# A two-layer graph network on one core: the transposes of h move from TensorE to VectorE and a DRAM table

## The reference

```python
h = jnp.maximum(_layernorm(x, axis=-1), 0.0)       # 50000 x 256
agg = jax.ops.segment_sum(h[src], dst, num_segments=50000)
h = agg + h
h1 = h @ W1 + b1                                    # 256 -> 1024
mean = jnp.mean(h1, axis=0)
var = jnp.mean(jnp.square(h1 - mean), axis=0)
h1 = relu((h1 - mean) * rsqrt(var + 1e-05) * gamma + beta)
out = x + relu(h1 @ W2 + b2)                        # 1024 -> 256
```

## Time and profile before

| what | value |
|---|---|
| median of 3 runs | 3976.13 us (3973.02 to 3977.18) |
| the profiled execution, its own time | 3966.72 us |
| its span, first to last instruction | 3965.0 us |
| PE busy | 3512.4 us, 89% |
| DVE busy | 2160.1 us, 54% |
| ACT busy | 2164.0 us, 55% |
| POOL busy | 1039.5 us, 26% |
| mean granted clock of TensorE | 0.950 |

### The profile page before, as it was taken

How to read it: one execution, slowest core, us unless ns; L and a number is a source line. 1 busy time by engine, 2 the same in 40 slices (tenths; PEclk the granted TensorE clock), 3 DMA queues, 4 the chain that set the end, 5 groups by cost and what they waited for, 6 DMA issues and landing times.

```text
span 3965.0 us, 58120 instructions
## 1 busy us (share of the span) xinstructions
PE 3512.4 (89%) x17911; PEld 2992.4 (75%) x17911; DVE 2160.1 (54%) x5128; ACT 2164.0 (55%) x3631; POOL 1039.5 (26%) x801
## 2 busy tenths in 40 slices
PE   0388887678777699999999999999999999999999
PEld 0377776567666577688888888888888888888888
DVE  0366665566565588745545555554555555555554
ACT  0255554222222299855666666566656666666665
POOL 6478887788888500000000000000000000000000
PEclk9888888888888799999999999999999999999999
DMA  9978886677776799712122222112112221221220
GB/s 338 333 191 192 194 197 112 164 159 165 160 160 156 174 360 360 292 49 63 64 79 63 63 70 73 63 63 79 64 63 68 74 63 63 78 65 63 68 75 32
DMA packets 172573, 517.28 MB, mean 130 GB/s; under 512 B 26133, under 2 KB 78352, under 8 KB 166576
## 3 DMA queue, kind: packets, MB, share of 16 engines
q1 hardware_dynamic: 96160, 412.93, 30.5%
q0 software_dynamic: 75264, 102.81, 15.2%
q10 hardware_dynamic: 1072, 0.76, 0.1%
HBM read 361.58 MB, written 206.03 MB: 143 GB/s over the span
## 4 chain that ended last, share of the span: by engine, by line
PE 58%; POOL 19%; issue 9%; DMA 7%; ACT 5%; DVE 1%; ACTq 0%; POOLq 0%; SPq 0%; DVEq 0%
PE ps_a L1216 27%; PE ps_b L1230 18%; PE ps_b L1231 9%; POOL x_table L499 7%; POOL agg_table L499 6%; POOL arena L489 5%; DMA x_table<-in_x 4%; ACT arena L632 4%; PE ps_a L1200 2%; DMA agg_table<-arena,scatter_now 2%; DMA x_table<-arena,scatter_now 1%; ACT arena_r L650 1%; DMA arena<-x_table,gather_ids 0%; PE ps_a L1179 0%; ACT arena L578 0%
## 5 line engine op out<-in xcount | busy, mean ns | idle before, releaser
L1216 PE MATMUL ps_a<-arena_r 128*128 128x512 f32 (+1 forms) x4704 | 1196.6, 393 | 1.5 <-DVE arena_r L1039 1.5
L1230 PE MATMUL ps_b<-arena_r 128*128 128x512 f32 x3128 | 1138.6, 398 | 0.1
L1047 DVE TENSOR_TENSOR arena_r<-arena,arena_r 128x512 fp32r<-128x512 f32 (+1 forms) x784 | 540.0, 689 | 958.2 <-ACT arena_r L689 958.2
L684 ACT ACTIVATE arena<-ps_a,bn_bias,bn_scale 128x512 f32<-128x512 f32 (+1 forms) x784 | 606.1, 773 | 780.3 <-PE ps_a L1216 760.1
L1216 PEld LDWEIGHTS ps_a<-arena_r 128*128 128x128 f32 x4704 | 834.9, 188 | 177.7 <-ACT arena_r L675 1.9
L1231 PE MATMUL ps_b<-arena_r 128*128 128x256 f32 x3128 | 876.4, 280 | 0.0
L1230 PEld LDWEIGHTS ps_b<-arena_r 128*128 128x128 f32 x3128 | 587.1, 188 | 132.1 <-issue 0.4
L1231 PEld LDWEIGHTS ps_b<-arena_r 128*128 128x128 f32 x3128 | 590.3, 189 | 27.3
L689 ACT ACTIVATE arena_r<-arena 128x512 fp32r<-128x512 f32 (+1 forms) x784 | 494.6, 631 | 71.8
L1127 PE MATMUL ps_b<-arena,arena_r 128*128 128x256 f32 x1568 | 407.1, 425 | 0.0
L632 ACT ACTIVATE arena<-arena,norm_now 128x256 f32<-128x256 f32 (+1 forms) x782 | 403.6, 587 | 3.5 <-DVE norm_now L938 3.5
(11 more groups left out here) (116 smaller groups left out, 3863.4 us busy)
## 6 DMA issues: line engine op xcount, KB each, us to landing
arena<-x_table SPq DMA_DIRECT2D x291, 512.0 KB, 3.7
arena<-agg_table SPq DMA_DIRECT2D x194, 512.0 KB, 5.2
x_table<-in_x SPq DMA_DIRECT2D x10, 5000.0 KB, 32.8
agg_table<-zeros SPq DMA_DIRECT2D x40, 1250.0 KB, 5.5
out<-zeros SPq DMA_DIRECT2D x97, 512.0 KB, 6.0
arena<-in_x,gather_ids POOLq DMA_INDIRECT x196, 14.3
x_table<-arena,scatter_now POOLq DMA_INDIRECT x196, 4.1
arena<-x_table,gather_ids POOLq DMA_INDIRECT x196, 2.9
```

Of the source, the lines that this page charges most:

```text
L684: act.activation(hid[m % 2][:, 0:w], ps_a[:, 2 + m % 2, 0:w], ACT.Relu, scale=bn_scale[:, m:m + 1], bias=bn_bias[:, m:m + 1]).then_inc(hid ...
L1047: dve.tensor_tensor(hid_lo[m % 4][:, 0:w], hid[m % 2][:, 0:w], hid_hi[m % 4][:, 0:w].bitcast(F32), ALU.subtract).then_inc(hid_lo_ready, 1)
L1216: ins = pe.matmul(ps_a[:, 2 + m % 2, 0:w], w_part[:, kb, cols], h_part[:, kb, 0:w], start=(t == 0), stop=(t == len(terms) - 1))
L1230: pe.matmul(ps_b[0:p, r, :], hid_hi[m % 4][:, cols], w2, start=(m == 0), stop=(m == MB - 1), skip_group_check=True)
```

## The change

**In the node stage** PE no longer transposes. `add_agg` writes h so that the four rows' pieces of 32 features lie side by side; `turn_squares` on DVE transposes every square of 32 partitions by 32 columns in place (`dve.transpose`, 128x1024 in one instruction); and SP (`turn_h`) stores the four bands of 32 partitions into a DRAM table `hT_table` in runs of 128 floats (512 bytes, 256 runs a band), waits until they have landed, and loads the table back as features by nodes into `hT_f` (512 KB). ACT takes the high part of it in one operation of 1024 columns (`take_hT`), and DVE the low part (`hT_low`), both from SBUF. The nodes of a chunk come back in another order, which ACT puts right when it reads the hidden block out of PSUM: its source pattern now has runs of 32 columns. All of it is for a chunk ahead: `prepare` is done two chunks ahead, in two halves after blocks 3 and 4; `add_agg` two ahead after block 7; `turn_squares` one ahead after block 0; `finish` moves from block 1 to block 2; `take_hT` and `hT_low` one ahead after block 6. The last chunk is computed 384 nodes wide, not 336.

**In the batch norm** DVE adds `w1_cov[1]` to `w1_cov[0]` (one operation of 1024 columns), and PE sums only the result, in 8 matmuls, not 16. Chunk 0 is turned while PE is still in the batch norm, and chunk 1 is prepared there.

**In memory** the two big tiles are split into separate ones with the same use; the edge stages and the Gram pass keep their instructions and order.

```diff
+            def turn_h(n, s, k):
+                s2 = s % 2
+                columns = width(n) // BANDS
+                sp.wait_ge(turned_ready, n + 1)
+                by_band = hT_table[s2].rearrange("(c e) t -> e c t", e=SQUARE)
+                for a in range(BANDS):
+                    rows = h_turned[s2][a * SQUARE:(a + 1) * SQUARE, :].rearrange("e (c t) -> e c t", c=CB)
+                    sp.dma_start(by_band[:, :, a * columns:(a + 1) * columns], rows[:, :, 0:columns]).then_inc(hT_stored[s2], 16)
+                sp.wait_ge(hT_stored[s2], 16 * BANDS * (turn_of(s, k) + 1))
+                sp.dma_start(hT_f[s2][:, 0:KB * width(n)].rearrange("p (k t) -> p k t", k=KB),
+                             hT_table[s2][:, 0:width(n)].rearrange("(k p) t -> p k t", p=P)).then_inc(hT_loaded[s2], 16)
...
+                for u in range(1, LOADS + 1):
+                    here = LOADS * i + u, u % LOADS, i + u // LOADS
+                    turn_h(*following(*following(*here)))
+                    load_and_store(*here)
...
+            def take_hT(n, s, k):
+                columns = KB * width(n)
+                act.wait_ge(hT_loaded[s % 2], 16 * (turn_of(s, k) + 1))
+                act.activation(hT_hi[s % 2][:, 0:columns], hT_f[s % 2][:, 0:columns], ACT.Copy).then_inc(hT_hi_ready, 1)
...
-                for kb in range(KB):
-                    act.wait_ge(hT_done, KB * n + kb + 1)
-                    act.activation(hT_hi[:, kb, 0:w], ps_a[:, kb, 0:w], ACT.Copy).then_inc(hT_hi_ready, 1)
...
+                    by_row = ps_a[:, 2 + m % 2, 0:w].rearrange("p (a r b) -> p r a b", a=BANDS, b=SQUARE)
+                    act.activation(hid[m % 2][:, 0:w].rearrange("p (r a b) -> p r a b", a=BANDS, b=SQUARE), by_row, ACT.Relu,
                                    scale=bn_scale[:, m:m + 1], bias=bn_bias[:, m:m + 1]).then_inc(hid_ready, 1)
...
+                    if m in (3, 4) and has(n, 2):
+                        prepare(*following(*following(n, s, k)), m - 3)
+                    if m == 6 and has(n, 1):
+                        take_hT(*following(n, s, k))
...
+            def turn_squares(n, s, k):
+                dve.wait_ge(h_ready, n + 1)
+                if not (isinstance(n, int) and n < 2):
+                    dve.wait_ge(hT_stored[s % 2], 16 * BANDS * turn_of(s, k))
+                dve.transpose(h_turned[s % 2][:, :], h[s % 2].rearrange("p j d -> p (j d)")).then_inc(turned_ready, 1)
...
+            dve.wait_ge(bn_act, 4 + KB)
+            dve.tensor_tensor(w1_cov[:, 0, :], w1_cov[:, 0, :], w1_cov[:, 1, :], ALU.add).then_inc(bn_act, 1)
...
-            def transpose_h(n, s):
-                p, j = shape_of(n)
-                pe.wait_ge(h_ready, n + 1)
-                for kb in range(KB):
-                    for r in range(j):
-                        ins = pe.transpose(ps_a[:, kb, r * p:(r + 1) * p], h[s % 2][0:p, r, kb * P:(kb + 1) * P], ident[0:p, 0:p])
-                    ins.then_inc(hT_done, 1)
...
+            def column_sums():
+                pe.wait_ge(bn_act, 5 + KB)
+                for m in range(MB):
+                    ins = pe.matmul(ps_b[:, 1, m:m + 1], w1_cov[:, 0, m * P:(m + 1) * P], ones[:, 0:1], start=True, stop=True)
+                ins.then_inc(bn_pe, 1)
```

More of the change, by code:

```diff
@@ L139, in gnn_program @@
[L139 to L147, removed]
@@ new lines, in gnn_program @@
+        w1_lo = sb("w1_lo", [P, KB, HID], F32R)[:, :, :]
+        w2_hl = sb("w2_hl", [P, MB, 2, D], F32R)[:, :, :, :]
+        node_std = sb("node_std", [P, CHUNKS, ROWS])
+        node_rstd = sb("node_rstd", [P, CHUNKS, ROWS])
+        node_shift = sb("node_shift", [P, CHUNKS, ROWS])
+        hid = [sb(f"hid{s}", [P, CHUNK])[:, :] for s in range(2)]
+        h_turned = [sb(f"h_turned{s}", [P, SLOT]) for s in range(2)]
+        hT_f = [sb(f"hT_f{s}", [P, KB * CHUNK]) for s in range(2)]
+        SQUARE = 32
@@ L253, in gnn_program @@
         h_ready = sem("h_ready")
-        hT_done = sem("hT_done")
+        turned_ready = sem("turned_ready")
+        hT_stored = [sem(f"hT_stored{s}") for s in range(2)]
+        hT_loaded = [sem(f"hT_loaded{s}") for s in range(2)]
         hT_hi_ready = sem("hT_hi_ready")
@@ L321, in shape_of, with has, is_first, following @@
             return (TAIL_P, TAIL_ROWS) if isinstance(n, int) and n == CHUNKS - 1 else (P, ROWS)
+        def has(n, ahead):
+            return not isinstance(n, int) or n + ahead < CHUNKS
+        def is_first(n):
+            return isinstance(n, int) and n == 0
+        def following(n, s, k):
+            return n + 1, (s + 1) % LOADS, (k if s < LOADS - 1 else k + 1)
+        def width(n):
+            return shape_of(n)[1] * P
+        def turn_of(s, k):
+            return 2 * k + s // 2
         def halves(j):
@@ L963, in _, with hT_low @@
             pick_norm(1, 1)
+            def hT_low(n, s):
+                columns = KB * width(n)
+                dve.wait_ge(hT_hi_ready, n + 1)
+                dve.tensor_tensor(hT_lo[s % 2][:, 0:columns], hT_f[s % 2][:, 0:columns], hT_hi[s % 2][:, 0:columns].bitcast(F32),
+                                  ALU.subtract).then_inc(hT_lo_ready, 1)
             def add_agg(n, s, k):
@@ L991, in _ @@
             add_agg(0, 0, 0)
+            turn_squares(0, 0, 0)
             for i in range(KB):
@@ L1048, in main @@
                                       ALU.subtract).then_inc(hid_lo_ready, 1)
-                    if m == 1 and not first:
+                    if m == 0 and has(n, 1):
+                        turn_squares(*following(n, s, k))
+                    if m == 2 and not first:
                         finish(n - 1, (s - 1) % LOADS)
-                    if m == 5 and not (isinstance(n, int) and n == CHUNKS - 1):
-                        add_agg(n + 1, (s + 1) % LOADS, (k if s < LOADS - 1 else k + 1))
-                    if m == 2 and not (isinstance(n, int) and n + 2 >= CHUNKS):
-                        pick_norm(n + 2, s % 2)
+                    if m == 4 and has(n, 3):
+                        pick_norm(n + 3, (s + 1) % 2)
+                    if m == 6 and has(n, 1):
+                        hT_low(n + 1, s + 1)
+                    if m == 7 and has(n, 2):
+                        add_agg(*following(*following(n, s, k)))
+            add_agg(1, 1, 0)
+            pick_norm(2, 0)
             main_schedule(dve, main, loop=lambda passes, body: looped(passes, 2 * LOADS, body))
```

192 lines of the change are left out of this document (99 added, 93 removed).

## The result

The changed kernel takes **3889.06 us**, median of four runs (3888.09 to 3891.04), beside 3976.45 for the kernel before, measured with it (3973.02 to 3977.18): a ratio of 0.9783, 95% interval 0.9766 to 0.9799. The forecast was 3889, range 3879 to 3930.

A forecast was written before the change was run, and what follows sets the result against it. PE, busy 600.00 of 600 us in the node stage, was taken to bound the kernel; 81.6 us from its transposes plus 5 from batch norm and chunk 0 made 86.6, off the median 3976.13: 3889 us, range 3879 to 3930.

The forecast's parts named there:

- PE's stream: Node stage: removing PE's transposes saves 0.79 + 0.06 = 0.85 us a chunk, 81.6 us over chunks 1 to 96.
- Batch norm and chunk 0: Before the node stage: half the column sums and chunk 0 turned beside them start `up(0, 0)` 5 us earlier (3.5 to 6.1).
- (a): `turn_squares` on DVE after block 0: takes 1.22 us, and may take up to 2.4 before PE waits for `down(n, 1)`.
- (b): SP's stores and load back of turned h: 5 us to land, 3.6 to load; there at 2314.7, bounds 2312.4 and 2317.2.
- (c): `take_hT` on ACT between blocks 6 and 7: 1.09 us, fits whole if the load has landed by 2316.7.
- (d): PE's cover ahead of `down(n-1, 7)`, behind block 7's low part: 0.24 us left where 1.1 were.
- (g): ACT reading hidden blocks in runs of 32 columns: 0.78 us if free; 0.1 us too much costs 9.7 us in all.
- (e): DVE at the chunk's end: `hT_low` ends before low part 7, and `add_agg` fits before `read_down` with 0.1 us to spare.
- (f): `prepare` in halves in ACT's gaps, and chunk loads some 5 us later: cost nothing; SP's round fills 18 of 22.3 us.
- Rival 1: Node stage: the bounce misses its deadline at 0.128 us a run, every chunk waits 1.6 us, 4045 us; chance 0.08.
- Rival 2: Node stage: long squares, hidden blocks or `add_agg` exceed their cover, 0.1 to 0.5 us a chunk, 3899 to 3937 us; chance 0.10.
- Rival 3: Node stage: something else holds the chunk at 23.1 us, only the batch norm's 5 us show, 3971; chance 0.03 with similar cases.

The follow-up runs named there:

- pe_turn_back: The changed kernel with eight transposes of a constant, read by nobody, put back on PE at the head of each chunk: 3971.83 us, ratio 0.999.
- bounce_two_more: The changed kernel with the load of `hT_f` done three times, each waited for before the next: 4123.76 us, ratio 1.0371 to the kernel before.
- squares_thrice: The changed kernel with DVE's transpose of the squares done three times, each waited for: 3987.53 us, ratio 1.0048 to the kernel before.

## Why the prediction was right, by its steps

- **PE's stream.** Taken 0.85 us a chunk, 81.6 in all; measured 0.83 (23.15 to 22.32) and 79.8. 96 x 0.83 = 79.7, so the difference is the 0.02 by which the 0.06 behind the transposes was read too large, and the last chunk gave nothing, as assumed. The mechanism is shown by **pe_turn_back**.
- **Batch norm and chunk 0.** Taken 5 of 3.5 to 6.1, measured 5.9 (6.9 in the second trace of the changed kernel). The bounce's speed decides here as well: ACT had `hT_f` before the sums ended, near the best end of the bounds. The 1.8 us missing above and the 0.9 won here leave 85.7 of 86.6; that the total met 3889 to a tenth of a microsecond is luck within the scatter.
- **(a) Squares.** 1.24 us for the 1.22 taken; cover 2.7 for 2.4.
- **(b) The bounce.** The mis-sized term. I took 5 us from the last issue to the landing of the stores; they landed 3.9 us after the *first* issue, 2.5 each. The load's 3.6 was right. PE's slack was 5.1 where I had 2.3. The bound from below, 2.7 for a store of 336 KB in long runs, was the near one. The Trainium skill (DMA: Bandwidth & Descriptors, Specifications) gives 512 bytes as the least transfer at line rate. The trace agrees as far as it goes: 512 KB in such runs, as four stores, were down 3.9 us after the first issue, and a load of 512 KB in long runs takes 3.6; no run has the same stores in long runs.
- **(c)** ACT took the high part whole, 1.05 us, with no wait; where it does wait, PE stops ahead of `down(n-1, 7)`: **bounce_two_more**.
- **(d), (g) Cover of block 7.** 0.24 predicted, 0.23 in the rows of after read in the same way, 0.19 to 0.20 by experiment; PE takes DVE's end 0.11 to 0.12 us later and not 0.04. It did not matter, for the hidden block stayed at 778 ns. Had it been 0.1 us longer it would have cost nothing; 0.3 longer, some 10 us.
- **(e)** `add_agg` ends at 2322.78 and `read_down` starts at 2323.01, with 0.23 to spare. `hT_low` ends 0.6 before low part 7.
- **(f)** The halves of `prepare` and the later loads: no cost seen. The loads land slower (x1 4.5 and the sums 6.1 us, in place of 3.6 and 5.3), with DMA at 0.38, and nobody waits for them.
- **Rival 1** was right in its mechanism and place, wrong in its price: 0.128 us a run of the edge stages' indirect transfers does not hold for a direct store. 64 runs an engine in at most 3.9 us are 0.061 us each at most. It also left out what **bounce_two_more** shows, that some of the waits are followed by a stretch at the 1.2 GHz level.
- **Rival 2** gave nothing; each of its covers exists and has an end, found by experiment. **Rival 3** fell with **pe_turn_back**.
- **The rule that speaks against it.** PE's price for turning h is 0.83 us, less than DVE's 1.24 alone. The Trainium skill (VectorE: DVE Perf Modes, Rules for kernel authors) says to use TensorE for a 128x128 transpose where PSUM will do as destination. By the engines' own prices the trace agrees, and the path that replaces it takes 8.8 us (2304.64 to 2313.4). It wins here because PE has no idle time and nobody waits for the other path.

What stays open: the cover of 0.15 by rows against 0.19 to 0.20 by experiment in (d) differs by more than one row is rounded, and I did not separate PE's hand-over from a few hundredths that PE makes up elsewhere in the chunk.

## What to carry to other kernels

When one engine is busy all the time, price a step by that engine's time alone, and give every piece of the replacement a deadline on the timeline; here a path ten times as long as the step it replaced cost nothing. Then test each cover from the side: lengthen one step until the time moves, and read in the trace how much the edit really delayed the next dependent instruction, since an added operation that depends on nothing overlaps both neighbours. Where a wait is followed by a lower granted clock, take the two apart before you work out a slack. Measure stages from a common event inside the program, not from the span's start, when an earlier stage scatters by as much as the effect.

## What the runs showed of the hardware that I had not expected

- A store of 128 KB from SBUF to DRAM in runs of 512 bytes lands in 2.5 us, four issued together in 3.9; the 512 KB read back take 3.6, and a dependent round of load and wait 3.5 on SP.
- DVE's transpose of 128x1024 float32 in 32x32 squares takes 1.24 us, where an addition of that shape takes 1.22.
- ACT reads PSUM in runs of 32 columns at no price: 778 ns for 512 columns, with 0.78 us in the earlier trace rows for contiguous ones.
- An independent operation put between two dependent ones on ACT adds less than its length: 0.40 us added 0.11, 0.62 added 0.33, and 1.05 added 0.76, always 0.29 less.
- With PE waiting some 2 us in each chunk, 20 of 85 chunks had a stretch at the 1.2 GHz level behind the wait, which cost 1.4 us each (**bounce_two_more**). In **squares_thrice**, with waits of 0.9 us, the granted clock stayed at 1.00.
- PE's weight load follows DVE's end by 0.11 to 0.12 us, DVE follows ACT's end by 0.04.
